# Mamba and MoE kernel, one core: the z products made and parked together, their silus spread over the gate groups, the next x transposed at the end of a pass, and GpSimd's y addition moved

## What is computed

```python
x = x + layernorm(mamba(layernorm(x)))
x = x + layernorm(moe(layernorm(x)))
# mamba: x_in, z = split(x @ W_in)              512 channels each
#   u = silu(conv4(x_in) + b); dt, B, C = split(u @ W_xproj)
#   delta = softplus(dt @ W_dt + b_dt); A = -exp(A_log)
#   h[t] = exp(delta * A) * h[t-1] + delta * u * B      16 states
#   y = sum_n h * C + D * u;  out = (y * silu(z)) @ W_out
# moe: out = sum over 2 shared and the top 2 of 8 experts of
#   (silu(x @ gate) * (x @ up)) @ down, experts weighted by softmax
```

## Time and profile before

| | us |
|---|---|
| median of 3 executions | 2432.21 |
| the profiled execution | 2430.07 |
| its span, first to last instruction | 2428.1 |
| busy: VectorE / TensorE / GpSimd / ScalarE | 2228.7 / 2073.8 / 1906.6 / 1601.1 |
| mean granted TensorE clock | 0.938 of 2.4 GHz |
| pass 8, from its first scan to that of pass 9 | 1187.36 to 1331.10, 143.74 |

### The profile page before, as it was taken

The page is one execution under the profiler, slowest core; times in us unless marked ns, Lnnn a source line. Parts: engine busy times, 40 slices in busy tenths (PEclk is TensorE's granted clock), DMA queues, the critical chain, the costliest instruction groups (busy, mean ns, idle before and its releaser), DMA issues. The chain is left out here.

```text
span 2428.1 us, 29696 instructions
## 1 busy us (share of the span) xinstructions
PE 2073.8 (85%) x8960; PEld 1322.8 (54%) x8960; DVE 2228.7 (92%) x3176; ACT 1601.1 (66%) x2358; POOL 1906.6 (79%) x1566
## 2 busy tenths in 40 slices
PE   5668989889898988989888898888989898896977
PEld 2445555656555555655655555555555555564544
DVE  3999999999999999999999999999999999998950
ACT  4556767676776767777677676667677676675632
POOL 3576887969789696978969788796978879698844
PEclk9659999999999999999999899999999999998989
DMA  4111211111121121111211121121112111111101
GB/s 135 34 34 42 70 53 57 58 49 57 53 62 57 49 57 58 57 53 58 65 46 47 58 65 55 55 57 50 56 53 62 61 49 53 49 57 48 65 23 44
DMA packets 92943, 134.23 MB, mean 55 GB/s; under 512 B 12000, under 2 KB 42976, under 8 KB 92784
## 3 DMA queue, kind: packets, MB, share of 16 engines
q1 hardware_dynamic: 92784, 132.34, 18.2%
HBM read 123.13 MB, written 9.18 MB: 54 GB/s over the span
## 5 line engine op out<-in xcount | busy, mean ns | idle before, releaser
L753 DVE TENSOR_TENSOR_SCAN h<-d_a,carry,d_bu 128x512 f32<-128x512 f32 x1024 | 1262.0, 1267 | 35.8 <-ACT d_a L602 35.4
L987 POOL TENSOR_TENSOR d_bu<-delta_u,b_rows 128x1024 f32<-128x1024 f32 x512 | 1202.3, 2357 | 5.1 <-DMA b_rows<-b_rows_hbm 0.9
L602 ACT ACTIVATE d_a<-delta,a_neg 128x512 f32<-128x512 f32 x1024 | 696.4, 689 | 622.2 <-DVE h L753 620.2
L445 PE MATMUL ht<-ident,h 128*128 128x128 f32 x4096 | 618.1, 295 | 116.8 <-DVE y_t L763 111.8
L445 PEld LDWEIGHTS ht<-ident,h 128*128 128x128 f32 x4096 | 503.7, 151 | 367.5 <-issue 132.0
L763 DVE SCALAR_TENSOR_TENSOR y_t<-ht,c_t,y_t 128x512 f32<-128x512 f32 x960 | 665.5, 734 | 2.8 <-PE ht L445 2.6
L509 PE MATMUL ring<-x_t,w_gate_sb 128*128 128x512 f32 x640 | 329.1, 641 | 20.6 <-ACT delta L718 19.1
L516 PE MATMUL ring<-x_t,w_up_sb 128*128 128x512 f32 x640 | 296.4, 606 | 23.0 <-ACT silu_gate L671 22.8
L536 PE MATMUL dn<-w_down_sb,hidden 128*128 128x256 f32 x1280 | 304.3, 381 | 13.2 <-POOL hidden L1045 13.2
L1040 POOL TENSOR_TENSOR hidden<-silu_gate,up 128x512 f32<-128x512 f32 x160 | 204.3, 1277 | 135.8 <-ACT up L675 77.9
L536 PEld LDWEIGHTS dn<-w_down_sb,hidden 128*128 128x128 f32 x1280 | 236.0, 190 | 74.8 <-issue 31.8
(11 more groups left out here) (111 smaller groups left out, 1868.7 us busy)
## 6 DMA issues: line engine op xcount, KB each, us to landing
b_rows<-b_rows_hbm SPq DMA_DIRECT2D x256, 256.0 KB, 3.5
coef_rows<-coef_rows_hbm SPq DMA_DIRECT2D x128, 256.0 KB, 3.5
xa<-L_attn_x_in SPq DMA_DIRECT2D x16, 512.0 KB, 5.1
xr<-L_attn_x_in SPq DMA_DIRECT2D x16, 512.0 KB, 5.2
out<-xr SPq DMA_DIRECT2D x16, 512.0 KB, 2.9
w_in_sb<-L_attn_W_in_in SPq DMA_DIRECT2D x1, 1024.0 KB, 6.4
w_gate_sb<-L_ffn_experts_gate_in SPq DMA_DIRECT2D x2, 512.0 KB, 4.5
w_up_sb<-L_ffn_experts_up_in SPq DMA_DIRECT2D x2, 512.0 KB, 5.4
```

What stands on the lines that cost most here:

```text
L445: last = nc.tensor.transpose(HT[q % HTS][:, j * P:(j + 1) * P], H[:, (NS * c + n) % HS, j, a * P:(a + 1) * P], IDN[:, :])
L602: nc.scalar.activation(DA[i % DAS][:, :], DL[:, r, j, :], ACT.Exp, scale=ANEG[:, j, n:n + 1]).then_inc(ex.sem, 1)
L753: nc.vector.tensor_tensor_scan(H[:, (NS * s + n) % HS, j, :], DA[(n * J + j) % DAS][:, :], BU[:, (2 * n + j // 2) % 4, j % 2, :], CARRY[:, ...
L987: nc.gpsimd.tensor_tensor(BU[:, (2 * n + h) % 4, :, :], DU[:, 2 * h:2 * h + 2, :], BB[:, n % 2, :].unsqueeze(1).to_broadcast([P, 2, T]), A ...
```

## The change

1. All four z products are made in slot 9, into the two dn banks in turn; ScalarE copies them unchanged into the tile silu_z (slots 8, 8, 9, 9; counted by a new semaphore z_raw), and the silus are done in place in that tile, one behind each pair of gate silus (slots 24, 34, 44, 52). The transpose of the normed residual waits for the four copies instead of two silus. In the first preparation, which has no scan beside it, all four z silus come in slot 11.
2. The silus of u, blocks 0 and 1, go from slot 8 to slot 7.
3. x of the chunk after next is transposed in slot 58 and copied in slot 59 (before: slots 0 and 1 of the next pass).
4. On GpSimd the addition of y stands in slot 8 behind o's row factors (before: slot 7), and gate_y stands ahead of slot 4's inflow.
5. On VectorE the moments of the expert result in slot 60 stand behind that slot's y additions; the moments of the next x are spread over slots 26, 32, 36 and 42 with their end in slot 46 (before: two in 32, two and the end in 42), and its row factors on GpSimd go from slot 44 to 47.

```diff
-        Y_POOL = 7
+        Y_POOL = 8
-        XA_STATS, XA_RSTD, XA_NORM = (32, 32, 42, 42), 44, 49
+        XA_STATS, XA_MEAN, XA_RSTD, XA_NORM, XT_PE, XT_ACT = (26, 32, 36, 42), 46, 47, 50, 58, 59
-        Z_PE, Y_STATS = (9, 9, 60, 61), 60
-        SILU = {8: [("u", 0), ("u", 1), ("z", 0), ("z", 1)], 11: [("u", 2), ("u", 3)], 62: [("z", 2), ("z", 3)]}
+        Z_PE, Z_ACT, Y_STATS = 9, (8, 8, 9, 9), 60
+        SILU = {7: [("u", 0), ("u", 1)], 11: [("u", 2), ("u", 3)], 24: [("z", 0)], 34: [("z", 1)],
+                44: [("z", 2)], 52: [("z", 3)]}
+        SILU_FIRST = {7: SILU[7], 11: SILU[11] + [("z", j) for j in range(J)]}
...
                 if t == X1T_PE:
                     if exists(lo + 1):
-                        pe.wait_ge(sz.sem, sz.at(s + 1, 2))
+                        pe.wait_ge(z_raw.sem, z_raw.at(s + 1))
...
-                    if t == Z_PE[j]:
+                    if t == Z_PE:
                         if j < 2:
                             pe.wait_ge(resid["o"].sem, resid["o"].at(s - 1, 2 * j + 2))
                         else:
-                            pe.wait_ge(*ring_user_before(s, lo, "z", j))
+                            pe.wait_ge(z_raw.sem, z_raw.at(c, j - 1))
...
+                for j in range(J):
+                    if t == Z_ACT[j]:
+                        act.wait_ge(full["z"].sem, full["z"].at(c, j + 1))
+                        act.wait_ge(y_gate.sem, y_gate.at(s - 1))
+                        nc.scalar.activation(SZ[:, o, j, :], DN[j % 2][:, :], ACT.Copy).then_inc(z_raw.sem, 1)
...
-                    if with_scan and n + 1 < NS and t % 2 == 0:
-                        inflow(s, n + 1, t % NT // 2)
-                    if ffn and t == 60:
-                        rstd_of("y", s - 1)
                     if ffn and t == Y_GATE:
                         for j in range(J):
                             gate_y(s - 1, o, j)
+                    if with_scan and n + 1 < NS and t % 2 == 0:
+                        inflow(s, n + 1, t % NT // 2)
+                    if ffn and t == Y_STATS:
+                        rstd_of("y", s - 1)
```

More of the change, by code:

```diff
@@ L415, in body @@
                         prep_part(s, lo, 1 - r, t)
+                    if exists(lo + 2) and t == XT_PE:
+                        x_t(s, lo)
             def x_t(s, lo):
-                pe.wait_ge(norm["xa"].sem, norm["xa"].at(s + 1))
+                pe.wait_ge(norm["xa"].sem, norm["xa"].at(s + 2))
                 for k in range(KM):
@@ L543, in prep_part @@
                 c = s + 1
-                if t == 0:
-                    x_t(s, lo)
                 for j in range(J):
@@ L650, in body @@
                         normed("xa", s + 2, XA, XA)
+                    if exists(lo + 2) and t == XT_ACT:
+                        for k in range(KM):
+                            act.wait_ge(full["xt"].sem, full["xt"].at(s + 2, k + 1))
+                            act.wait_ge(full["z"].sem, full["z"].at(s + 1))
+                            nc.scalar.activation(XT[:, k, :], ring_bank("xt", k)[:, :], ACT.Copy)\
+                              .then_inc(xt.sem, 1)
             def ffn_part(s, lo, o, t):
@@ L684, in prep_part @@
                 c = s + 1
[L685 to L689, removed]
                 for j in range(J):
@@ L700, in prep_part @@
                           .then_inc(tap0.sem, 1)
-                for what, k in SILU.get(t, ()):
+                for j in range(J):
[3 more added lines that the diff above has]
+                        nc.scalar.activation(SZ[:, o, j, :], DN[j % 2][:, :], ACT.Copy).then_inc(z_raw.sem, 1)
+                for what, k in (SILU if exists(lo) else SILU_FIRST).get(t, ()):
                     if what == "u":
@@ L705, in prep_part @@
                     else:
[L706 to L708 removed]
+                        act.wait_ge(z_raw.sem, z_raw.at(c, k + 1))
+                        nc.scalar.activation(SZ[:, o, k, :], SZ[:, o, k, :], ACT.Silu).then_inc(sz.sem, 1)
                 if t == XD_PE + 1:
@@ L814, in body @@
                             moments("xa", s + 2, a, XA[:, a, :])
-                            if a == NT - 1:
-                                moments_end("xa", s + 2)
+                    if exists(lo + 2) and t == XA_MEAN:
+                        moments_end("xa", s + 2)
+                    if ffn and t == Y_STATS:
+                        dve.wait_ge(down.sem, down.at(s - 1))
+                        for a in range(NT):
+                            moments("y", s - 1, a, dn(a))
+                        moments_end("y", s - 1)
             def over(t):
@@ L885, in ffn_part @@
                             route(c, 8 * half + 2 + i)
[L886 to L890, removed]
             def conv_part(c, o, t):
```

12 lines of the change are left out of this document (5 added, 7 removed).

## The result

The changed kernel takes **2450.94 us** (median of four runs, 2450.29 to 2453.09) against 2432.15 us for the kernel before on the same chip: a ratio of 1.0079, interval 1.0062 to 1.0096. It is 18.8 us slower. The forecast was 2453 us, with its own range of 2445 to 2460 (2434 to 2468 with the rivals).

The account below looks back on a forecast made before the run. VectorE's instruction list was taken as the bound. A full pass: -0.5 + 0.9 + 1.25 = +1.65 us, times 14 +23; opening and end -1.8; +21 on 2430.07, median 2.1 above: 2453 us, range 2445 to 2460 (2434 to 2468 with rivals).

Parts of the forecast that it names:

- Slot 60, -1.25 us: VectorE's 1.2 us wait for the last down product goes, with two y additions ahead of y's moments; -1.25 us a pass.
- Slot 9, -0.95: VectorE's wait of 1.3 us for o's row factors from GpSimd falls to 0.35; -0.95 us a pass.
- Slots 7 to 14, -0.5 left at full clock: A ScalarE and TensorE chain delays scan 14's decay: -0.5 of 2.2 us is left, with a 2 us wait there.
- The clock, +0.9 out of 0 to 1.8: Slots 61 to 4: TensorE's clock is down when the y transposes start, delaying the chain; +0.9 us a pass.
- a sign that I had named against myself: The forecast is wrong if the first x_in records of a pass are 0.43 us apart.
- Gate groups, +1.25: Slots 24, 34, 44, 52: a third silu adds 0.52 us to each group; with moved moments, +1.25 us of waits a pass.
- Opening, +3: More z work in the first preparation +3.7, next x's transposes and copies +2.4, a 3.12 us wait gone; net +3 us.
- End, -4.8: Passes 15 and 16: waits for o's row factors shrink by 2.2 and about 1.4, slot 60 gives 1.2; -4.8 us.
- Rival A: TensorE's clock holds at 2.4 GHz through the moved transposes and states: 2441 us; chance 0.20.
- Rival B: The chain of slots 7 to 14 has more slack, so the 2.2 us are kept: 2417 us; chance 0.13.
- D: Gains and losses cancel within 0.2%: 2432 us; chance 0.07.
- C: TensorE's clock comes back late in every pass and holds o's moments too, +1.8 instead of +0.9: 2466 us; chance 0.13.

Follow-up runs that it names:

- the filler: Changed kernel with ten more transposes of a constant tile in each of TensorE's slots 60 to 63, 0 and 1: 2440.7 us, ratio 1.0037.
- version 5: Kernel before with GpSimd's two moves and y's moments behind slot 60's additions, next x's moments where they were: 2398.8 us, ratio 0.987.
- version 4: Kernel before with GpSimd's two moves, y's moments behind slot 60's additions and the next x's moments spread: 2399.6 us, ratio 0.9868.
- version 8: Changed kernel with x's transposes put back into slot 0 of the next pass and their copies into slot 1: 2438.6 us, ratio 1.0034.
- version 7: Changed kernel with the copies of z blocks 2 and 3 cut from 512 columns to 16: 2438.1 us, ratio 1.0032.

## Why the prediction was right, and where it was off

**Slot 60, -1.25 us: right.** The wait was 1.20 us and is gone, in all but pass 14. On top of GpSimd's moves it is worth 20 to 21 us.

**Slot 9, -0.95: right.** 1.29 fell to 0.31 (0.35 was forecast), for the reason given: the row factors on GpSimd now come ahead of the addition. Only in pass 1 had there been no such wait to win.

```profile
1221.49 0.21 POOL L957 TENSOR_TENSOR var_eps_o<-mean_var_o,eps 128x4 f32<-128x4 f32 x1
...
1223.02 2.36 POOL L980 TENSOR_TENSOR xr<-xr,silu_gate 128x1024 f32<-128x1024 f32 x1
```

**Slots 7 to 14, -0.5 left at full clock: right in kind, 0.35 us too dear.** My chain put the decay of scan 14 at 41.1 us behind the first scan (1227.2 in rows' time, with the pass starting 1.25 earlier), and the wait at 2.0 us. At full clock, with the filler, the scan starts at 41.46, so its decay of 0.7 at 40.7, and the wait is 1.65.

**The clock, +0.9 out of 0 to 1.8: right in the mean, with luck.** The out projection starts between 12.60 us (as with the filler) and 14.21, in the mean 0.79 us later than with the filler, and 0.7 us a pass is what putting x's transposes back gives (the 14 full passes take 2021.3 instead of 2031.0 us). I had taken the middle of the bounds as a constant; it is a mean of passes in which the clock is back before, within or behind the y transposes. Nothing in the rows put the mean in the middle. The upper bound was also summed wrongly: its terms (2.1 us more for the y transposes, less 2.2 of waiting, 2.7 more for x_in) make 2.6, not 1.8, and their middle would have been 1.3; the latest out projection came 1.6 us late. And a sign that I had named against myself did show: in seven of the 14 full passes (2, 3, 6, 8, 10, 12 and 14) x_in's records are 0.43 us apart from the second on, as in the passes with filler. There the clock costs only what the y transposes lose, or nothing.

**Gate groups, +1.25: right.** The waits in slots 27, 37, 47 and 55 are 0.38, 0.38, 0.43 and 0.71 (forecast 0.35, 0.38, 0.3 and 0.7), those behind the softplus 0.04 each (forecast 0.13). Against the 0.73 of before this is +1.24.

So a full pass was forecast 1.65 us longer, and is 1.26: 2013.3 us became 2031.0 over the 14 passes. The step mis-sized is that of slots 7 to 14 with its clock, +0.4 in the forecast; the waits of slots 9, 11, 14 and 60 together changed by -0.07 a pass. Most of the 0.4 is the chain at full clock, 0.35 us shorter than I had it.

**Opening, +3: right.** The first scan starts at 56.59 instead of 50.51 us, the +6.1 of the forecast (3.7 and 2.4), the wait of 3.12 is gone, and pass 1 starts 3.13 us later. With x's transposes back the first scan starts at 54.02, so the two parts are 3.5 and 2.6.

```profile
56.59 8.33 DVE L757 TENSOR_TENSOR_SCAN h<-d_a,carry,d_bu 128x512 f32<-128x512 f32 x7 [17.73 <-ACT d_a L601]
```

**End, -4.8: wrong, it is 0.** From the first scan of pass 15 to the end it is 233.9 us in both. VectorE's last scan does come 2.8 us sooner, but not by the waits that I had listed. The one for o's row factors in pass 15 shrank from 2.5 to 1.9 only, where I had it shrink by 2.2; that of slot 60, 1.2, went as forecast; a wait of 2.1 us for the out projection in slot 8, which I hadn't listed, went too, and others grew. The wait for the same row factors in pass 16, which I had going, was 1.48 us and is 1.47. Behind the last scan the closing took 2.8 us more: the y transposes and the out projection ran at the lower clock. TensorE, kernel before and then changed:

```profile
2334.85 1.10 PE L458 MATMUL ring<-ident,y_t 128*128 128x128 f32 x8 [0.84 <-DVE y_t L763]
...
2338.38 7.14 PE L469 MATMUL dn<-w_out_sb,y_d 128*128 128x256 f32 x32 [1.55 <-POOL y_d L1033]
```

```profile
2352.85 1.97 PE L459 MATMUL ring<-ident,y_t 128*128 128x128 f32 x8 [0.84 <-DVE y_t L767]
...
2357.41 9.00 PE L470 MATMUL dn<-w_out_sb,y_d 128*128 128x256 f32 x32 [0.89 <-POOL y_d L1037]
```

```profile
2353.00:2363.00 10.00, 9.12 (x33) 7.80 (x34) 2.99 (x4) 0.00 (x0) 4.94 (x4) 0.59 0.00 0
```

I had counted the clock's price in the passes and forgotten it at the end, where no scans hide TensorE. It isn't tied to the change alone: version 5, with z as before, has the slow closing too (out projection 8.88 us, 101.3 us from the last scan to the end), version 4 hasn't (7.14 and 99.1). Two errors of opposite sign, -5.5 over 14 passes and +4.8 at the end, cancel; that the total came so close is partly luck.

Rival A (the clock holds, 2441) is what the filler shows, at 2440.7: its price was right and its condition false. Rival B (the 2.2 us are kept) failed at its own test: the decay had to start 39.1 us into the pass and came at 41.5. D (no change) is out, as the ratio's interval ends at 1.0062. C would need an out projection 14.4 us into every pass; the latest single one was 14.21.

What z's part costs, 39 to 40 us, can be read between version 5 and version 8: a full pass is 2.8 us longer, 1.34 by the wait in slot 14 and 1.25 by those behind the gate and softplus groups. Taking parts out doesn't give these shares back, since other waits step in: the silus left out bring 26.3 us in the changed kernel and 15.2 in version 8, where slot 60 takes more. What stays open is how the 1.34 us divide between the order of z behind the fourth first_state, the two further products and the copies: version 7 shows 0.5 for two copies, and a version with z of blocks 2 and 3 back in slots 60 and 61 wasn't run. And why the clock comes back now in the y transposes, now behind them, the runs don't say.

## What to carry to other kernels

A saved wait is worth what the next serial chain lets through: here 2.2 us won on VectorE in slots 60 and 9 met a chain over ScalarE and TensorE that the same change had made longer. List that chain step by step before filling an engine's idle time with "free" work, and test parts of a change alone; two small moves without the rest were worth some 32 us, the whole cost 19. And work on an engine with idle time isn't always dead weight: eight transposes in the right slot brought TensorE's clock back to 2.4 GHz early in the pass, filler kept it there, and either gave 10 to 12 us.

## What was not expected of the hardware

The granted clock settled into a pattern of two passes: 0.57 and then 1.00 from 9 us into one pass, 0.50 and 0.72 in nearly the same stretches of the next, with identical work in both. Each late return made the pass 1.1 us longer. With x's eight transposes at the head of a pass (in pass 8 granted 0.74 over the first 5 us, 1.00 behind) this pattern is gone and the out projection starts between 12.60 and 13.25 us, while state transposes alone left the clock at 0.50 for those 5 us in all passes but one (0.63 in pass 3). That activity releases the clock is what the Trainium skill (TensorE: Matmul & The Clock Gate, Part 1) says; the rows add that TensorE needn't stand idle to be held at its lower level: it was busy for 49 of the 75 us at 0.52, and for 3.56 of the 5.20 us at 0.50 above.
